# A gated attention and expert kernel: batch 0 attends first, and its expert blocks run in between the other batches' attention steps

## The reference

```python
# gated attention, all batches; 16 heads of 128 columns; context of 512 rows of 256
q, k, v = x_norm @ Wq, ctx @ Wk, ctx @ Wv          # per head
q, k = rmsnorm(q, gq), rmsnorm(k, gk)
attn = softmax(q @ k.T / sqrt(128))
x = x + tanh(g_xattn[1]) * ((attn @ v) over all heads) @ Wo
# mixture of experts: 16 experts of 352 inner columns, 4 per token; 512 tokens
h = silu(xs @ gate[e].T) * (xs @ up[e].T)
y = h @ down[e].T                                  # weighted and added to its token
x[0] = x[0] + tanh(g_ffn[1]) * sum of the four y
```

## Time and profile before

| | |
|---|---|
| time, median of 3 runs | 1653.09 us (1653.08 to 1655.2) |
| the profiled execution's own time | 1654.8 us |
| its span, first to last instruction | 1653.0 us |
| mean granted TensorE clock | 0.97 of full speed |
| busy: TensorE, VectorE, ScalarE, GpSimd | 1512.6, 1057.6, 962.9, 704.9 us |
| DMA traffic | 122.91 MB |

### The profile page before, as it was taken

One profiled execution on the slowest core, in us unless ns is written; L12 is line 12 of the kernel. 1 busy time (PEld: TensorE's weight loads), 2 busy tenths in 40 slices (PEclk: granted clock), 3 DMA queues, 4 the chain that ended last, 5 costly groups with the idle time before them and its releaser, 6 DMA issues.

```text
span 1653.0 us, 26231 instructions
## 1 busy us (share of the span) xinstructions
PE 1512.6 (92%) x8413; PEld 1273.6 (77%) x8413; DVE 1057.6 (64%) x1999; ACT 962.9 (58%) x2160; POOL 704.9 (43%) x614
## 2 busy tenths in 40 slices
PE   5879899999999999999999999999999868878881
PEld 4768778888888888888888888888888756767771
DVE  7776566666666666666666666666666655565553
ACT  6854456656656566566565565665655446556560
POOL 3444223343433333334343343343433335775755
PEclk9999889999999999999999999999999989999996
DMA  6300000000000000000000000000000268898884
GB/s 233 118 33 13 1 7 14 8 13 19 6 13 6 13 13 13 13 6 13 13 13 13 6 13 13 13 13 6 13 6 0 91 229 315 302 317 311 301 287 146
DMA packets 39389, 122.91 MB, mean 74 GB/s; under 512 B 4464, under 2 KB 4464, under 8 KB 39344
## 3 DMA queue, kind: packets, MB, share of 16 engines
q1 hardware_dynamic: 35584, 110.03, 19.0%
q0 software_dynamic: 3760, 12.32, 2.8%
HBM read 108.96 MB, written 13.37 MB: 74 GB/s over the span
## 4 chain that ended last, share of the span: by engine, by line
PE 67%; DMA 8%; POOL 8%; issue 7%; DVE 6%; ACT 4%; SPq 1%; ACTq 0%; POOLq 0%; DVEq 0%
PE j_bank L393 10%; PE j_bank L395 10%; PE j_bank L394 10%; PE t_bank L474 6%; DMA x_sb<-w_gu 6%; PE w_bank L393 5%; PE w_bank L395 5%; PE w_bank L394 5%; PE s_bank L393 4%; POOL cT_lo L1264 3%; PE s_bank L395 3%; PE s_bank L394 3%; PE t_bank L543 2%; DMA xn<-w_gu 1%; PE t_bank L555 1%
## 5 line engine op out<-in xcount | busy, mean ns | idle before, releaser
L756 ACT ACTIVATE prob<-s_bank,neg_bias,q_scale 128x512 f32<-128x512 f32 x256 | 198.3, 776 | 307.7 <-DVE neg_bias L1106 307.5
L890 DVE TENSOR_TENSOR probT_lo<-t_bank,probT_hi 128x512 fp32r<-128x512 f32 x264 | 176.4, 689 | 207.1 <-ACT probT_hi L669 207.1
L1124 DVE SCALAR_TENSOR_TENSOR x_sb<-w_bank,inv_sum,x_sb 128x512 f32<-128x512 f32 x256 | 184.8, 743 | 1.4 <-PE w_bank L395 1.4
L1096 DVE TENSOR_REDUCE neg_max<-s_bank 128x1 f32<-128x512 f32 x256 | 169.1, 681 | 6.6 <-PE s_bank L395 6.6
L474 PE MATMUL t_bank<-ident,prob 128*128 128x128 f32 x1024 | 154.6, 274 | 8.0 <-ACT prob L756 6.0
L1340 POOL TENSOR_TENSOR k_ms<-k_ss,eps 128x4 f32<-128x4 f32 x64 | 12.9, 202 | 346.3 <-ACT xn L800 346.3
L669 ACT CAST probT_hi<-t_bank 128x512 fp32r<-128x512 f32 x264 | 149.9, 594 | 1.8 <-PE t_bank L474 1.6
L393 PE MATMUL j_bank<-wkv_lo,cT_hi 128*128 128x256 f32 x512 | 146.0, 285 | 2.6 <-issue 1.6
L1264 POOL TENSOR_TENSOR sqs_lo<-xn,sqs_hi 128x512 fp32r<-128x512 f32 x64 | 83.8, 1310 | 144.8 <-ACT xn L817 144.8
L395 PE MATMUL j_bank<-wkv_hi,cT_lo 128*128 128x256 f32 x512 | 145.1, 283 | 0.0
L394 PE MATMUL j_bank<-wkv_hi,cT_hi 128*128 128x256 f32 x512 | 144.8, 283 | 0.0
(11 more groups left out here) (239 smaller groups left out, 4504.2 us busy)
## 6 DMA issues: line engine op xcount, KB each, us to landing
x_sb<-w_gu SPq DMA_DIRECT2D x46, 704.0 KB
stage<-w SPq DMA_DIRECT2D x48, 256.0 KB, 2.6
prob<-w_dn SPq DMA_DIRECT2D x16, 768.0 KB, 5.3
stage<-w_dn SPq DMA_DIRECT2D x15, 768.0 KB, 6.2
xn<-w_gu SPq DMA_DIRECT2D x16, 704.0 KB
planes<-bits SPq DMA_DIRECT2D x16, 512.0 KB, 4.0
y<-x_sb SPq DMA_DIRECT2D x31, 256.0 KB
x_sb<-x SPq DMA_DIRECT2D x4, 1024.0 KB, 10.4
```

The lines of the kernel that those rows point to most:

```text
L756: nc.scalar.activation(prob[:, i, :], s_bank[i % 2][:], ACT.Exp, bias=neg_bias[:, u % 2, i:i + 1], scale=q_scale[:, u % 2, i:i + 1], accum ...
L890: return nc.vector.tensor_tensor(dst, src, hi, ALU.subtract)
L1096: nc.vector.tensor_reduce(neg_max[:, u % 2, i:i + 1], s_bank[i % 2][:], AX_X, ALU.max, negate=True).then_inc(own_max, 1)
L1124: nc.vector.scalar_tensor_tensor(out=here, in0=w_bank[i % 2][:], scalar=inv_sum[:, w % 2, i:i + 1], in1=here, op0=ALU.mult, op1=ALU.add).t ...
```

## The change

The 64 items of attention are put in another order: first batch 0 over all 16 heads (items 0 to 15), then for each head batches 1, 2 and 3 (items 16 to 63). All steps are unrolled, and a step is numbered t: it projects item t, scores item t - 1 and finishes item t - 2. In step T0 - 2 = 18 batch 0 is normalised; block b of the experts runs in step t = 20 + b, its down product in step 21 + b. Steps 20 to 51 are called packed. In these `project_out` uses one PSUM bank (w_bank[0], shared with down), and the block's rows, gate, up and inner transposes the other (w_bank[1]). Gate and up weights are laid out anew in two halves of 176 inner columns, each half with gate and up side by side: `gate_up(0)` and `gate_up(1)` are 12 products of 352 columns. A chunk of weights (a half, or down) has one of two areas in turn; on-the-fly splitting is ScalarE for all hi parts, VectorE for the lo part of half 0, GpSimd for the lo parts of half 1 and of down. Down is 6 products of 512 columns and 6 of 256. Batch 0 waits in DRAM (x0_dram) meanwhile; the y rows are gathered in steps 52 to 55 and added in steps 54 to 57. The weights of a head are loaded whenever the head changes (`fresh(t)`): at each of items 0 to 15 and then at every third item, 32 times in place of 16, and wo is now cast behind the second softmax of its step.

```diff
+ITEMS = [(h, 0) for h in range(H)] + [(h, b) for h in range(H) for b in range(1, B)]
+NI = len(ITEMS)
+T0 = H + 4
+def fresh(t):
+    return 0 <= t < NI and (t == 0 or ITEMS[t][0] != ITEMS[t - 1][0])
@@ SyncE
+            for t in range(NI + 2):
+                b = t - T0
+                if fresh(t):
+                    key_weights(SET[t] + 1)       # waits for wkv_lo of step t
+                    query_weights(SET[t] + 1)     # waits for wq_lo of step t
+                if 0 <= b < NB:
+                    gate_up_weights(b, 1, e)      # waits for d_mm of block b - 1
+                if 0 < b <= NB:
+                    y_store(b - 1)
+                if fresh(t - 2):
+                    out_weights(SET[t - 2] + 1)   # waits for wo_lo
...
+                if 0 <= b < NB:
+                    down_weights(b, e)            # waits for a_mm of block b
+                if 0 <= b < NB - 1:
+                    e = expert(b + 1)
+                    gate_up_weights(b + 1, 0, e)  # waits for b_mm of block b
@@ TensorE, step(t)
+                    need(pe, w_added, 4, w, i if packed else i - 1)
+                    product(w_bank[0 if packed else i % 2][:], [a[:, i * P:(i + 1) * P] for a in oT],
...
                 scores(0)
                 scores(1)
                 query_squares()
+                turn_rows()
+                project_down()
                 values()
                 key_value(0)
                 probs(0)
                 scores(2)
+                gate_up(0)
                 key_value(1)
                 project_out(0)
                 scores(3)
                 probs(1)
                 query((0, 1))
+                if packed:
+                    project_out(1)
                 probs(2)
+                gate_up(1)
                 query((2, 3))
+                if packed:
+                    key_turn()
+                    project_out(2)
+                    turn_inner()
+                    probs(3)
+                    project_out(3)
@@ ScalarE, step(t)
+                if t and fresh(t):
+                    split_wkv(t)
+                gate_up_hi(0)
+                softmax(0)
+                if not packed:
+                    values_hi()
+                softmax(1)
+                rows_to_hi()
+                if fresh(w):
+                    split_wo(w)
+                if t and fresh(t):
+                    split_wq(t)
+                if packed:
+                    values_hi()
+                key_value_rows(0)
+                probs_hi(0)
+                if packed:
+                    gate_up_hi(1)
+                    softmax(2)
+                    silu(0)
+                    key_value_rows(1)
+                    key_squares()
+                    softmax(3)
...
                 probs_hi(1)
+                down_hi()
                 probs_hi(2)
+                silu(1)
+                query_hi()
+                inner_hi()
                 probs_hi(3)
+                def silu(half):
+                    nc.scalar.activation(h_row[:, half * HALF:(half + 1) * HALF], w_bank[1][:, 0:HALF],
+                                         ACT.Silu).then_inc(silu_ready, 1)
@@ VectorE, step(t), packed
+                maximum(0); maximum(1); squares_out(); shift(0); shift(1)
+                gate_up_lo(); inverses(); copy_y(); rows_to_lo(); take(0); values_lo()
+                probs_lo(0); maximum(2); shift(2); take(1); inner(0); values_rows(); add(0)
+                maximum(3); shift(3); take(2); probs_lo(1)
+                add(1); probs_lo(2); inner(1); query_lo(); key_lo(); add(2); inner_lo(); add(3); probs_lo(3)
@@ GpSimd, step(t)
+                if t and fresh(t):
+                    lower_wkv(t)
+                query_scale()
+                if fresh(w):
+                    lower_wo(w)
+                if t and fresh(t):
+                    lower_wq(t)
+                if up:
+                    take_rows(b + 1)
+                gate_up_lo()
+                scale_keys()
+                values_lo()
+                down_lo()
+                squares_lo()
+                if 0 <= b - NB - 1 < NT:
+                    take_y(b - NB - 1)
```

More of the change, by code:

```diff
@@ L156, in flamingo_kernel @@
         idx = sb("idx", [P, NT, TOPK], I32)
-        idx_f = sb("idx_f", [P, NT, TOPK])
         topw = sb("topw", [P, NT, TOPK])
         pair_w = sb("pair_w", [P, PAIRS])
[L160 to L168, removed]
+        h_row = sb("h_row", [P, HW])
         pair_slot = sb("pair_slot", [P, PAIRS], I32)
@@ L178, in flamingo_kernel @@
         w0s = oT
+        idx_f, token, count, blocks, first, ends, slot_f, block_f, pos_f = (
+            h_row[:, PAIRS * n:PAIRS * (n + 1)] for n in range(9))
+        block_e = h_row[:, PAIRS * 9:PAIRS * 9 + NBW]
         expert_of = routes[:, 2, 0:PAIRS * E].rearrange("p (c e) -> p c e", c=PAIRS)
@@ L323, in _, with weights, key_weights, query_weights @@
-            with sp.Fori(1, H) as h:
-                head_weights(h)
+            def weights(n, which, arrived, used):
+                if n >= SETS:
+                    return
+                wait(sp, used, n)
+                sp.dma_start(stage[:, which, :], w1[which, SET_HEAD[n]]).then_inc(arrived, 16)
+            def key_weights(n):
+                weights(n, 0, wkv_in, wkv_lo)
+            def query_weights(n):
+                weights(n, 1, wq_in, wq_lo)
+            def out_weights(n):
+                weights(n, 2, wo_in, wo_lo)
@@ L368, in _ @@
[L368 to L385, removed]
@@ L876, in _ @@
-            inner_to_hi(NB - 1)
+            for t in range(NI + 2):
+                step(t)
         @block.vector
@@ L1087, in _, with step @@
                                                        op1=ALU.add).then_inc(bit_added, 1)
[L1089 to L1090 removed]
+            def step(t):
+                u, w, b = t - 1, t - 2, t - T0
+                proj, score, value = t < NI, 0 <= u < NI, w >= 0
+                up, down = 0 <= b < NB, 0 < b <= NB
+                packed = up or down
+                combine = b - NB - 3
                 def maximum(i):
@@ new lines, in add, with query_lo @@
+                    here = x_sb[:, ITEMS[w][1], i, :]
+                    nc.vector.scalar_tensor_tensor(
+                        out=here, in0=w_bank[0 if packed else i % 2][:], scalar=inv_sum[:, w % 2, i:i + 1],
+                        in1=here, op0=ALU.mult, op1=ALU.add).then_inc(w_added, 1)
+                def query_lo():
+                    if not proj:
+                        return
+                    need(dve, q_hi, 1, t, 1)
+                    lower(qT[1][:, t % 2, :], j_bank[1][:], f32(qT[0][:, t % 2, :])).then_inc(q_lo, 1)
@@ new lines, in copy_y, with rows_to_lo @@
+                def copy_y():
+                    if not down:
+                        return
+                    dve.wait_ge(d_mm, b)
+                    wait(dve, y_out, 16 * (b - 1))
+                    nc.vector.tensor_copy(y_row, w_bank[0][:]).then_inc(y_copied, 1)
+                def rows_to_lo():
+                    if not up:
+                        return
+                    dve.wait_ge(rows_hi, b + 1)
+                    lower(rowT[1], w_bank[1][:], f32(rowT[0])).then_inc(rows_lo, 1)
@@ new lines, in inner, with inner_lo @@
+                def inner(half):
+                    if not up:
+                        return
+                    dve.wait_ge(silu_ready, 2 * b + half + 1)
+                    here = h_row[:, half * HALF:(half + 1) * HALF]
+                    nc.vector.tensor_tensor(here, w_bank[1][:, HALF:2 * HALF], here, ALU.mult).then_inc(h_ready, 1)
+                def inner_lo():
+                    if not up:
+                        return
+                    dve.wait_ge(h_hi, b + 1)
+                    lower(hT[1], w_bank[1][:, 0:HW], f32(hT[0])).then_inc(h_lo, 1)
@@ L1165, in step @@
                 shift(3)
+                take(2)
                 probs_lo(1)
[L1167 to L1180 removed]
```

979 lines of the change are left out of this document (483 added, 496 removed).

## The result

The change makes the kernel slower: **1700.91 us** (median of 4 runs, 1691.91 to 1708.98) beside 1654.14 us before on the same chip (4 runs, 1653.08 to 1657.68). The ratio is 1.0277, 95% interval 1.0219 to 1.0336. The forecast was 1701. The profiled execution is the fastest of the four (own time 1691.91, span 1690.1), so what follows is read against the forecast span, whose parts add up to 1700.6, and the other runs lie up to 17 us above what the trace shows. A ratio leaves out runs that lie over 1.5% above the fastest of their kernel; in this document these are three of the ten runs of e3.

The account below looks back on a forecast made before the run. TensorE was taken to bound attention, and weight loading the expert blocks. 1301 us to step 64, plus 217 expert work, 150 packed-step waits, 8 gathers and 24.4 tail gave 1701 us; range 1670 to 1735.

Parts of the forecast that it names:

- Start and pitch: Start unchanged, q_ss of step 4 at 265.56; plain steps 17.21 us, expert work on TensorE 7.0 us a block.
- Layer norm of batch 0: Normalising batch 0 among the early steps was put at 1 us.
- (a): Packed steps: project_out(3) waits for VectorE's add(2), queued behind key_lo; 0.95 us a step.
- (b): Exp/Silu table loads, four a packed step; silu(1)'s reaches TensorE: stall 2.7 us, (a) included. V is query_squares' end.
- (c): Port tie: GpSimd's subtraction may hold VectorE's shift(2) (neg_bias) 3 us; stall 5.7 for 2.7, in half the steps.
- (d): SP's queue: in 10 new-head packed steps gate_up(1)'s load waits behind query_weights; 5.8 us stall each.
- The clock: Half-clock spells after gaps of over 2.5 us, only in the upper bound: up to 40 us more.
- Gathers: Gathers of y on GpSimd in steps 52 to 55, ahead of the next q_scale: 8 us (0 to 15).
- rival 1: Silu costs no table switch, or its switches are hidden; milder (d): 1626 us, chance 0.14.
- Rival 2: Table loads stay, but VectorE wins the port tie and the queue does little: 1637 us, chance 0.15.
- Rival 3: Every shift(2) is caught and gaps halve the clock repeatedly: 1743 to 1783 us, chance 0.2.
- Rival 4: TensorE-bound as intended, with only (a) as stall in packed steps: 1580 us, chance 0.06.

Follow-up runs that it names:

- e3: The changed kernel with the next head's wq load issued behind gate_up(1)'s load and y's store in SyncE's order: 1650.84 us, ratio 0.9931.
- e8: e4 with the edits of e6 and e7 together: 1553.9 us, ratio 0.9396 to the kernel before.
- e6: e4 with add(2) put ahead of key_lo on VectorE in the packed steps: 1561.25 us, ratio 0.9441.
- e5: e4 without its Silu part, so e2 and e3 together with Silu and its 124 table loads: 1614.8 us, ratio 0.9757.
- e4: The changed kernel with the edits of e2 and e3, and Silu made of Tanh without table switches: 1586.65 us, ratio 0.9587.
- e1: The changed kernel with Tanh in place of Silu (another function), so no table switches: 1652.75 us, ratio 0.9984.
- e2: The changed kernel with neg_bias made by tensor_scalar, q_scale as scalar operand, instead of a two-input tensor_tensor: 1669.61 us, ratio 1.0089.
- e7: e4 with the gathers of y issued right behind query_scale instead of behind squares_lo: 1576.65 us, ratio 0.9535.

## Why the prediction was right, and where its terms were off

In the profiled execution, against the sum (us):

| stretch | forecast | measured |
|---|---|---|
| to q_ss of step 4 | 265.6 | 264.9 |
| steps 4 to 19 | 16 x 17.21 + 3 = 278.4 | 282.0 |
| packed steps 20 to 51 | 32 x 17.21 + 217 + 150 = 917.7 | 898.6 |
| steps 52 to 63 | 12 x 17.21 + 8 = 214.5 | 221.5 |
| tail | 24.4 | 23.0 |
| span | 1700.6 | 1690.1 |

- **Start and pitch: right.** The early steps take 17.3 where 17.21 was put: the 2 us for two more casts each. TensorE's expert work of 7.0 us a block is confirmed by e8: 24.1 - 17.3 = 6.8.
- **Layer norm of batch 0: too small.** Step 18 took 21.0 us and step 19 17.8, 4.2 over plain ones where 1 was put.
- **(a) right.** The chain stands in the rows, and e6 puts it at 0.79 a step; forecast 0.95.
- **(b) right in kind, too dear.** All 124 switches are there, and silu(1) is the one that reaches TensorE. But the walk gave 26.9 for a plain step and it is 25.6: a stall of 1.4 us over the 24.2, not 2.7. ScalarE was free from probs_hi(2) at 846.94, 17.9 us after the step's q_ss, which starts right behind V; the walk had V+19.8. Without tie and queue the loads are 28 us (e5 against e4). In the kernel as changed they are 48 (e1), where the forecast's terms said 75. The steps put the difference down to the tie: a caught step loses 28.8 - 25.6 = 3.2 us with the loads and 25.8 - 24.8 = 1.0 without them (six such steps in e1's execution), 2.2 x 9 = 20 us. No run has loads and tie without the queue beside one without the loads. That the loads behind a late softmax(2) have no idle time left to lie in is the likely reason, and isn't shown apart.
- **(c) right, place and size; the count is luck in part.** The tie is a tie, it strikes 9 of 21 steps (11 of 22 assumed), and a caught step costs 3.2 (forecast 3.0). But 6 of the 12 that escape do so by a late transfer and not by the toss that "half of the steps" stood for. e2 removes it without moving a transfer, so it is the two-input form, and not the timing, that is held up. That the spread of the runs (17 us, some 5 or 6 caught steps) comes from it is supported, not shown for single runs: it is 6 us in e2 and 1.1 in e8, and 32 in e3, where the tie is open in more steps. It isn't all: e1 spreads by 15 us, though a caught step costs 1.0 there.
- **(d) right in place, and in size by errors that offset each other.** 30.7 for 30.0; e3 brings 27.2 and 50 us. The queue held the load to V+6.0 and not 7.5; the load took 4.5 to 4.9 us in four steps, as put, and 6.7 to 8.8 in six; the hold of a VectorE cast, 1.2 us a step in the sum, was some 0.2 (0.61 to 0.68 us beside GpSimd's subtraction, for 0.43).
- **The clock: put at nothing outside the upper bound.** A granted clock of 0.96 over 899 us is some 70 us at the lower level. Nine of the ten new-head steps have 2.9 to 6.1 us of it, and eight of the nine caught ones 3.2 to 3.4. The bound had it after gaps of over 2.5 us; the trace has it after 2.2 as well (step 21, below). What it cost in all no run shows apart, as the other waits take up some of it: caught step 21 had it and took 28.8 us, caught step 29 had none and took 28.7. In e4, which has none of these gaps, the clock of the packed steps is 1.00.
- **Gathers: too small, inside their bound.** Steps 52 to 57 take 14.3 us more than six of 17.21, for 8 (0 to 15). Their place accounts for 7.6 of it (e7); the rest wasn't taken apart. In step 53 (q_ss at 1463.59) q_scale comes 2.7 us behind q_ss instead of 0.2, because two gathers of the step before are still in GpSimd's way:

```profile
1464.10 0.95 POOL L1445 DMA_INDIRECT xnT_raw<-y,pair_slot  x1 [0.30 <-issue]
...
1466.33 1.04 POOL L1427 TENSOR_TENSOR q_scale<-q_ss,minus_half 128x4 f32<-128x4 f32 x1
```

So the agreement to 0.1 us is luck in part: the packed steps came 19 us under the forecast, the steps around them 11 over, and the profiled run is 9 below the median. The mechanisms and their rank stood up, and that decided the sign. With the measured rest of the span (1690.1 - 898.6 = 791.5) the break-even step is (1653.0 - 791.5) / 32 = 26.9; the forecast had 27.2. e2 (mean 27.2, ratio 1.0089) and e3 (26.6, 0.9931) lie on the two sides of it.

The rivals: rival 1's condition (no switch) is e1, 1652.75 where it gave 1626: the new-head steps gained nothing, which the rival's "milder (d)" had put at 1.8 each. Rival 2's condition is e5, 1614.8 where it gave 1637. Rival 3 would have needed every shift(2) caught. Rival 4 (1580) is near e4, and e8 goes below it since it has no term (a).

**What stays open.** The new-head steps don't gain in e1 because the load of gate_up(1) sets them: its cast starts no earlier for the missing table loads. Where the cast starts alike, so is the step: step 25 has it 10.4 us after q_ss in e1 and 10.6 in the changed kernel, and takes 28.6 and 28.7. But eight of the ten in e1 have it at 12.0 us or later, against six, and the lower clock lasts longer in them: in step 28 TensorE works on at 0.50 for 5.0 us (from 776.91), against 2.9. What decides either wasn't tried. Nor was e2 or e3 alone with e6's order.

## What to carry to other kernels

When two stages are merged, look at the mean step that breaks even, and then walk one merged step: here no engine was full, and five small waits (the three below, one addition's place and the gathers' place) decided between 1554 and 1701 us. The three are patterns: an activation function whose table differs from the one in use, put in the middle of a softmax pipeline; a tiny VectorE operation with two SBUF tensors beside a long GpSimd one (give it a scalar operand); a load that can go now, queued behind one that must wait. Waits compound, so test the fixes together as well as alone: the table loads were worth 48 us with the tie and the queue, and 28 without.

## What was unexpected of the hardware

- Of two operations that start at the same recorded time either can win: at 809.24 GpSimd's did, and VectorE's took 3.25 us; at 726.72 VectorE's took 0.16 us. The Trainium skill, "SBUF — State Buffer", section "Who interferes with whom", has whoever comes first hold the port; the trace agrees where the starts differ by more (step 30: VectorE 0.25 us ahead, 0.16 us; the earlier trace rows: GpSimd 0.07 ahead, 1.24 us), can't tell who came first where they don't, and adds that a length of one element doesn't help, and that the form with a scalar operand from SBUF isn't held (0.21 us in e2).
- A VectorE cast takes 0.56 us (step 30, from 841.12) where it runs into the end of GpSimd's subtraction (838.16 + 3.23 = 841.39), and 0.43 by itself (e2, 805.87): what that page says of the two-port mode, and small here. In e8, where the cast comes earlier in GpSimd's subtraction, it takes 0.85 us in most packed steps and up to 1.98 (step 21: from 580.20, GpSimd's ends at 580.76); the steps with 0.85 take 24.1 us all the same.
- The load of a table and the Silu behind it start 1.29 us apart (846.94, 848.23), with 1283 ns for the load; the drain that the Trainium skill, "ScalarE: Activation LUTs", section "What ACT_TABLE_LOAD costs", adds (1380 ns) wasn't seen here either.
- TensorE fell to its lower level in an idle stretch of 4.95 us, and stayed at the upper one after the 1.16 us of step 30 (clock 1.00 in a window from 851 to 855 us). Idle stretches of 2.21 us went both ways: behind the one of step 21 it worked at 0.50, behind that of step 29 at 1.00 (windows):

```profile
590.00:592.00 2.00, 2.00 (x8) 0.50 0.00 0
817.00:820.00 3.00, 3.00 (x20) 1.00 0.04 8
```
